# Second attention of a two-layer image transformer: scores and row maxima by halves of 64 rows, with four masked copies of the queries

## The reference

```python
h, s = 8, 16                     # HEADS, HEAD_DIM
q = (x @ Wq.T).reshape(b, t, h, s); k = (x @ Wk.T).reshape(b, t, h, s); v = (x @ Wv.T).reshape(b, t, h, s)
q = _layernorm(q, q_gamma, q_beta)          # over the 16 features of a head
k = _layernorm(k, k_gamma, k_beta)
scores = jnp.einsum('bqhs,bkhs->bhqk', q, k) / jnp.sqrt(s)
scores = jnp.where(cols > rows, -jnp.inf, scores)
attn = jax.nn.softmax(scores, axis=-1)
out = jnp.einsum('bhqk,bkhs->bqhs', attn, v).reshape(b, t, e)
return out @ Wo.T + bo
```

## Time and profile before

| | us |
|---|---|
| median of 3 runs | 2328.66 |
| lowest and highest | 2323.18, 2329.88 |
| profiled execution, its time | 2333.29 |
| its span in the profile | 2331.6 |
| PE busy | 1835.8 |
| DVE busy | 1339.7 |
| ACT busy | 1211.4 |
| POOL busy | 1161.9 |

### The profile page before, as it was taken

One profiled execution on the slowest core, in us unless ns is written; L12 is line 12 of the kernel. 1 busy time (PEld: TensorE's weight loads), 2 busy tenths in 40 slices (PEclk: granted clock), 3 DMA queues, 4 the chain that ended last, 5 costly groups with the idle time before them and its releaser, 6 DMA issues. The chain is left out here.

```text
span 2331.6 us, 48836 instructions
## 1 busy us (share of the span) xinstructions
PE 1835.8 (79%) x12709; PEld 1328.7 (57%) x12710; DVE 1339.7 (57%) x5135; ACT 1211.4 (52%) x2915; POOL 1161.9 (50%) x1035
## 2 busy tenths in 40 slices
PE   5888888872158874998797979797988459998996
PEld 3555555551136552665565656565655359998985
DVE  3788888855541104888777777777776422222222
ACT  2555555530025432876666666666665135555553
POOL 2344444413038872245545454545454448777776
PEclk8999999985569886999999999999999679999998
DMA  9777777610014332011111111111111057776775
GB/s 205 176 191 188 189 189 189 181 29 15 19 45 71 62 46 64 23 40 41 39 34 39 35 38 35 38 35 38 34 34 29 25 118 137 134 136 122 134 134 84
DMA packets 271687, 198.98 MB, mean 85 GB/s; under 512 B 26121, under 2 KB 251947, under 8 KB 271531
## 3 DMA queue, kind: packets, MB, share of 16 engines
q1 hardware_dynamic: 221547, 161.65, 26.8%
q0 software_dynamic: 49984, 35.38, 11.0%
HBM read 144.12 MB, written 52.80 MB: 84 GB/s over the span
## 5 line engine op out<-in xcount | busy, mean ns | idle before, releaser
L2123 POOL DMA_INDIRECT out_dram<-r_yw,r_idx x212 | 328.4, 1549 | 114.9 <-issue 50.4
L2015 POOL DMA_INDIRECT rows_scratch<-routed_row,slot_u x256 | 268.8, 1050 | 124.7 <-issue 72.8
L1691 ACT ACTIVATE a_probsT<-a_p_sc 98x392 f32<-98x392 f32 x384 | 191.9, 500 | 128.0 <-PE a_p_sc L1520 108.0
L2191 ACT ACTIVATE r_hT<-r_p_up,r_b1T 128x256 f32<-128x256 f32 x424 | 190.0, 474 | 115.0 <-PE r_p_up L2165 111.6
L2152 PEld LDWEIGHTS r_p_y<-w_all,r_hT 128*128 128x128 f32 x1696 | 223.3, 192 | 11.1
L2152 PE MATMUL r_p_y<-w_all,r_hT 128*128 x1696 | 224.2, 275 | 0.0
L2165 PE MATMUL r_p_up<-r_xgT,r_w1e 128*128 128x256 f32 x848 | 220.5, 383 | 0.7 <-ACT r_xgT L2196 0.6
L1517 PE MATMUL a_p_sc<-q_head,kT 128*98 128x392 f32 x512 | 218.9, 509 | 0.5 <-ACT q_head L1718 0.5
L407 PE MATMUL p_embed<-pix,w_pix 96*128 96x392 f32 x512 | 211.1, 520 | 4.8 <-ACT pix L533 4.8
L1718 ACT ACTIVATE q_head<-qT,head_of 128x196 f32<-128x196 f32 x512 | 197.1, 467 | 0.0
L650 POOL TENSOR_SCALAR vare<-mv 98x4 f32<-98x4 f32 x64 | 27.9, 436 | 296.9 <-DVE mv L628 215.7
(11 more groups left out here) (361 smaller groups left out, 4535.0 us busy)
## 6 DMA issues: line engine op xcount, KB each, us to landing
img<-in_x_dram SPq DMA_DIRECT2D x192, 196.0 KB, 3.6
img<-in_x_dram SPq DMA_DIRECT2D x192, 189.0 KB, 3.7
r_w1e<-in_L_ffn_W_dram SPq DMA_DIRECT2D x106, 256.0 KB, 3.0
r_xg<-rows_scratch SPq DMA_DIRECT2D x106, 130.0 KB
xn_scratch<-xn SPq DMA_DIRECT2D x32, 196.0 KB
h_scratch<-h SPq DMA_DIRECT2D x32, 196.0 KB
h<-h_scratch SPq DMA_DIRECT2D x32, 196.0 KB
h3b<-h_scratch SPq DMA_DIRECT2D x32, 196.0 KB
```

The source lines that it names most:

```text
L1691: act.activation(probsT[:, r3, m, b * 2 * PAIR:(b + 1) * 2 * PAIR], p_sc[i % 2][:, 0:2 * PAIR], ACT.Exp).then_inc(exped, 1)
L2015: pool.indirect_dma_start(rows_dram, bass.IndirectOffsetOnAxis(ap=slot_u[:, k % 2, c, t:t + 1], axis=0), row[:, k % 2, c, t, :], None).the ...
L2123: pool.indirect_dma_start(acc_dram, bass.IndirectOffsetOnAxis(ap=idx[:, (k - 3) % 4, t:t + 1], axis=0), yw[:, (k - 3) % 4, t, :], None, co ...
L2191: act.activation(hT[:, (k - 1) % 2, f, :], p_up[f][:, 0:G], ACT.Silu, bias=b1T[:, bass.ds(e * FC + f, 1)]).then_inc(act_h, 1)
```

## The change

The queries are written four times instead of once: `q_var[:, slot, v, :]` holds heads v and v+4 and zeros elsewhere, since ACT's activation multiplies and adds by `gains_var`, gains already masked. Partitions 0 to 63 hold heads 0 to 3 and partitions 64 to 127 heads 4 to 7, so that on either half of the partitions variant v has one head alone, and a matmul on 64 rows is exact for it. `q_head`, `k_head_b`, their masks and the bf16 copies are gone; the maxima are computed from the upper halves of the f32 words (`q_high`, `k_high`), read with a step of two.

Banks are handled two at a time: `score_pair(i)` and `max_pair(i)` fill both PSUM banks, one from rows 0 to 63 and one from rows 64 to 127, and wait until both were read. Banks are renumbered: 0 to 3 hold image 0, 4 to 7 the second tiles of both images (for the maxima the first tiles), 8 to 11 image 1. The pairs stand in TensorE's order at (0,1), (2,3), (4,5), (6,7), (8,9), (10,11); bank 6 moves behind the turning of `o_n`, and bank 8 behind the turning of queries and keys and the output projection. An f32 score pair has two matmuls of 392 columns, or four of 196; a maximum pair has four matmuls of 196 columns or eight of 98, and two mask matmuls; auxiliary matmuls are four a pair, 196 columns each. `weigh(0)` waits for 8 exponentials instead of 6.

```diff
-        qT = S("qT", [D, 2, COLS])
+        q_var = S("q_var", [D, 4, LIVE, COLS])
         kT = S("kT", [D, 4, COLS])
-        qT_b = S("qT_b", [D, 2, COLS], BF16)
-        kT_b = S("kT_b", [D, 2, COLS], BF16)
-        q_head = S("q_head", [D, HEADS, COLS])
-        k_head_b = S("k_head_b", [D, 2, HEADS, COLS], BF16)
+        q_high, k_high = q_var[:].bitcast(BF16), kT[:].bitcast(BF16)
...
+                def max_pair(i):
...
+                        done(pe, maxed, 12, u, i)
...
+                    for both in zip(*spans):
+                        for p, (rows, v, q0, k0, size, c) in enumerate(both):
+                            pe.matmul(p_max[p][:, c:c + size], high(q_high, rows, q4, v, (q0, TILE)),
+                                      high(k_high, rows, k4, (k0, size)), start=(c == 0), stop=False,
+                                      skip_group_check=True)
...
+                def score_pair(i):
...
+                        done(pe, exped, 12, u, i)
+                    s4 = (k - 3) % 4
+                    for x in range(2):
+                        for p in range(2):
+                            m, rows, var, _ = places(i + p)
...
+                            elif x == 0:
+                                o = m * PAIR
+                                pe.matmul(p_sc[p][:, 0:2 * PAIR], kT[rows, s4, o:o + TILE],
+                                          q_var[rows, s4, var:var + 2, o:o + PAIR], start=True, stop=False,
+                                          skip_group_check=True)
...
-                banks(4, 7)
+                banks(4, 6)
...
-                banks(7, 9)
+                banks(6, 8)
...
-                banks(9, 10)
+                banks(8, 10)
...
-                split(3, 1, 0, 2)
-                exps(2, 3)
-                split(3, 1, 2, 5)
-                exps(3, 4)
-                split(3, 1, 5, 8)
+                exps(2, 4)
...
+                    for v in range(LIVE):
+                        last = act.activation(q_var[:, (k - 1) % 4, v, :], p_q[0][:, 0:COLS], ACT.Identity,
+                                              bias=gains_var[:, v, 1:2], scale=gains_var[:, v, 0:1])
+                    last.then_inc(qT_ready, 1)
...
-                if on[2]:
-                    masked_keys()
                 maxes(0, 1)
...
+            dve.tensor_tensor(var_of[:], head_of[:, 0:LIVE], head_of[:, LIVE:HEADS], ALU.add).then_inc(wcp, 1)
+            dve.wait_ge(wcp, 2)
+            dve.tensor_tensor(gains_var[:], gains[:, 0:2].unsqueeze(1).to_broadcast([D, LIVE, 2]),
+                              var_of[:].unsqueeze(2).to_broadcast([D, LIVE, 2]), ALU.mult).then_inc(wcp, 1)
```

More of the change, by code:

```diff
@@ L1499, in max_bank @@
-                    last.then_inc(maxmm, 1)
-                def score_bank(i):
+                        done(pe, kT_ready, 1, u)
+                        done(pe, maxed, 12, u - 1)
+                    else:
+                        done(pe, maxed, 12, u, i)
+                    q4, k4 = (k - 2) % 4, (k - 2) % 4
+                    spans = []
+                    for p in range(2):
+                        m, rows, var, _ = places(i + p)
+                        if m is None:
+                            spans.append([(rows, var + j, x * PAIR, x * PAIR, TILE, (2 * x + j) * TILE)
+                                          for x in range(2) for j in range(2)])
+                        else:
+                            spans.append([(rows, var + j, m * PAIR + TILE, m * PAIR, PAIR, j * PAIR)
+                                          for j in range(2)])
@@ L1513, in score_bank @@
[L1513 to L1530, removed]
@@ L1531, in score_bank @@
-                    last.then_inc(scored, 1)
+                        done(pe, exped, 12, u - 1)
+                    else:
+                        done(pe, exped, 12, u, i)
+                    s4 = (k - 3) % 4
+                    for x in range(2):
+                        for p in range(2):
+                            m, rows, var, _ = places(i + p)
+                            if m is None:
+                                o = x * PAIR + TILE
+                                pe.matmul(p_sc[p][:, x * PAIR:(x + 1) * PAIR], kT[rows, s4, o:o + TILE],
+                                          q_var[rows, s4, var:var + 2, o:o + TILE], start=(x == 0), stop=False,
+                                          skip_group_check=True)
[3 more added lines that the diff above has]
+                                          q_var[rows, s4, var:var + 2, o:o + PAIR], start=True, stop=False,
+                                          skip_group_check=True)
@@ new lines, in score_pair @@
+                    for p in range(2):
+                        m, _, _, first = places(i + p)
+                        for par in range(2):
+                            head = aux_l[:, first + par, :]
+                            if m is None:
+                                bank = p_sc[p][:, 0:2 * PAIR].rearrange("p (x h c) -> p x h c", x=2, h=2)
+                                last = pe.matmul(bank[:, :, par, :], head, aux_r[:, r3, :, PAIR:3 * TILE],
+                                                 start=False, stop=True, skip_group_check=True)
+                            else:
+                                last = pe.matmul(p_sc[p][:, par * PAIR:(par + 1) * PAIR], head,
+                                                 aux_r[:, r3, m, 0:PAIR], start=False, stop=True,
+                                                 skip_group_check=True)
+                        last.then_inc(scored, 1)
@@ L1533, in banks @@
                 def banks(lo, hi):
-                    for i in range(lo, hi):
+                    for i in range(lo, hi, 2):
                         if on[3]:
-                            score_bank(i)
+                            score_pair(i)
                         if on[2]:
-                            max_bank(i)
+                            max_pair(i)
                 def qkv_tile(t):
@@ L1707, in tile @@
                              ).then_inc(qkv_act, 1)
[L1709 to L1720, removed]
                 if on[4]:
```

114 lines of the change are left out of this document (41 added, 73 removed).

## The result

The changed kernel takes 2389.4 us (median of 4 runs, 2380.9 to 2392.7), the kernel before, run beside it, 2329.3. The ratio is 1.0265 (95% interval 1.0240 to 1.0289), so it is **slower by 60 us**. I had forecast 2329 and a range up to 2352. The profiled execution has a span of 2379.2 us at a mean clock of 0.886; before it was 2331.6 at 0.904.

The account below looks back on a forecast made before the run. No engine is full; a chain of waits binds, POOL's ring at 27.45 us a unit. Steady units -5.4, jumps +7.5, units behind +5.4, head -3.8, tail -3 sum to +0.7: 2329 us on the median's scale, range 2296 to 2352.

Parts of the forecast that it names:

- The chain at full clock: Second attention, steady unit: the chain of waits between engines sets the time, 27.45 us before and 27.0 after.
- TensorE's ring: Second attention: chain of waits through TensorE and DVE, 25.5 us a unit plus 1.5 from the pairs, 27.0.
- rival A: The forecast itself: the pairs' addition to TensorE's ring takes back what scatters and banks give; 2321 to 2336, chance 0.33.
- B: Faster: DVE's second reduction is absorbed and POOL's 26.0 us ring binds; -33 us, 2296, chance 0.36.
- steady units: Twelve loop units, neither a jump's nor the next one: from 27.45 to 27.0 us each, -5.4 us in all.
- the six units behind the loop's start and its jumps: TensorE waits there for DVE, held 1.82 us in line 1936: 0.9 us lost each, +5.4 in all.
- rival C: Slower clock: if the hole before bank 7's maximum reaches 2.2 us, half the units pay 1.7; +20, 2350, chance 0.19.
- the 4.9 of the sum: TensorE's scores and maxima: the two 64-row halves run side by side and save 4.9 us a unit.
- The jump: Units at the loop's jump back, where POOL is long done, lose the pairs' 1.5 us in full: five, +7.5 us.
- The head: Units ahead of the loop, where TensorE is full and its ring not yet at its length: -3.8 us.
- a change of form: TensorE's switch between half and full rows, 24 a unit: 0.09 us each, 2.2 us a unit; ends 0 and 0.17.
- Rival D: The halves overlap in part (0.33 us a pair, +20, 2349) or not at all (+41, 2370); chance 0.12.

Follow-up runs that it names:

- the kernel with fillers: Changed kernel plus unread TensorE matmuls: six before the turn of the maxima, four before the routed rows, pair (6,7) scores twice; 2339.8 us, ratio 1.0058.
- moving the code: Changed kernel with eight tiny matmuls ahead of TensorE's stage program, nothing added in the loop; 2365.6 us, ratio 1.0159.
- eight copies: Kernel before with eight masked f32 query copies written by ScalarE, no VectorE masks, pairs or 64-row matmuls; 2314.7 us, ratio 0.9942; on the disturbed run 2521.6 us.

## Why the prediction was wrong

*The chain at full clock* was right in kind. TensorE's ring measures 27.12 us (27.0 foretold), the maxima stand 7.8 us behind the queries (7.5), all scatters are at 0.95, the rows no longer wait for rstd, the reduction of bank 0 binds. So rival A's mechanism is what the unit does, and B did not come. That the number fits so well is in part luck: behind bank 0 I had 7.8 - 1.9 = 5.9 us to the next reduction of head variance and there are 5.6, and for what the pairs add I had 1.5 us and there are 1.9 (1.3 up to the turn of the maxima, 0.7 at bank 0, less 0.1). With most of the clock and the second stop out of the way (the kernel with fillers, half clock 48 us, before 61), the loop takes 689.2 us against 694.6 before: steady units -6.8 in all (foretold -5.4), the jumps +6.4 (foretold +7.5), but the six units behind the loop's start and its jumps -5.0, where I had +5.4. I had kept VectorE's 1.82 us in line 1936 there, and they are gone.

*The clock* was the step that failed: the sum has no term for it, and it is worth about 26 us together with what it adds at the jumps. I had given rival C a condition, a single hole that reaches 2.2 us, and found 1.5 in the steady unit. The largest is 1.33, and yet half clock doubled. What the change did was to take work from TensorE (27.12 less its holes is 22.5 us, before 27.45 - 2.16 - 1.17 - 0.35 = 23.8; the 1.3 us are the 4.9 of the sum less 24 changes of 0.15) and to leave six holes, 0.45, 0.97, 0.50, 0.43, 1.33 and 0.98, where there had been three. One stretch at 0.50 after one long hole was too little to read a condition from; C was right in kind and, at 20 us, not far off in size; its condition was wrong.

*The jump* was the second step: +1.5 us each foretold, +4.9 measured. The difference is the second stop and half clock: moving the code brings the jumps to +2.6 each, the fillers to +1.3. The trace of before has no second stop at any jump. I had no bound for "the program's length changes".

*The head* was the third: -3.8 foretold, +11.5 measured. It has two parts. The first two intervals are 5.6 us longer; there TensorE stands 4.10 us, and once more 2.10, ahead of the maxima of a pair, behind reductions that lie among VectorE's root steps, where before the largest hole is 2.53, and half clock rises from 17 to 31 us.

```profile
920.17 0.57 PE L1499 MATMUL a_p_max<-kT,q_var 64*98 64x98 bf16 x8 [4.10 <-DVE a_negmax L1810]
```

The fillers come in only from the fourth interval on, so that the head is as long with them (+11.9) says nothing on the clock in these two; how much of the 5.6 us it is stays open. The other five intervals are 5.9 us longer, all at full clock; with eight copies and no pairs they are longer by 0.2, so this part comes with the pairs on half rows and not with the masked copies. Which of the two, pairs or half rows, isn't shown, and moving bank 1's reduction did not change it. I took TensorE for full in these units, which it is not.

*Mis-sized terms:* a change of form is 0.15 us, not 0.09. Leaving the masks out was worth 36 us, not 17: the twelve steady units give 14.0 us by the traces, but the units behind the loop's start and its jumps give 14.7 more, which I had not counted as going with the masks, and another 11 lie outside the loop. The weighting's 3.97 us should be 3.92, which changes nothing.

*Rival D* fell: records of both halves start 7 ns apart (1354.366 and 1354.373, then 1354.774 and 1354.781), so D's 0.33 us a pair don't come.

The accounts: of the 60 us the second stop is 24 and the clock 26, each to within about 10. The fillers' kernel still has 11 over the kernel before. Its profiled execution is the shortest of its six and only 2.6 us longer than that of before: 12 more in the head, 5 less in the loop, 4 less outside. The other 9 us are in no trace.

## What to carry to other kernels

A change that takes work from TensorE where it is not the bound can lose more clock than the work was worth, as here: look at all its holes in a unit, the small ones too, and price the units at half clock as a term, not as an accident. When a hardware loop's body changes its length, look at the first microseconds behind the jump back, on every engine, before anything else is explained. And when a change brings two things, here masks gone and halves paired, build the one without the other: the first alone made the kernel faster, by 0.6%.

## What the runs showed of the hardware

With matmuls on 64 rows, bank by bank, a unit has a single hole of over 0.3 us on TensorE (0.73, at the turn of the maxima). Half of the 24 intervals in the loop are 31.03 to 31.12 us without any half clock, and yet six take 41.7 to 51.6, of which 24 to 41 us are at 0.50. So a full engine alone doesn't keep the clock. That trace is of the longest of four executions whose times scatter; the shortest, 2537 us, is still above what units of 31.05 us would make (an estimate from the trace: 31.05 in place of the eight long intervals of head and loop and 40 a jump are some 134 us over the kernel before, so about 2460). Why, no other run here shows.

In two of the five batches, those where the kernel before took 2495 us, every unit from the sixth interval on was 6 to 8 us longer in the kernels traced. With eight copies the two conditions differ by 208 us in the profiled executions, 192 of them in the 31 intervals. It is always the same place, here in the kernel with eight copies:

```profile
1603.89 1.04 DVE L1808 TENSOR_REDUCE a_negmax<-a_p_max 98x2 bf16<-98x392 f32 x2 [5.97 <-remote]
1602.44 0.50 ACT L1695 ACTIVATE a_probsT<-a_p_sc 98x392 f32<-98x392 f32 x1 [4.08 <-remote]
1597.58 0.25 PE L1501 MATMUL a_p_max<-mask_qk,ident_b 98*98 98x196 bf16 x1
1605.06 0.41 PE L1668 MATMUL a_p_tr<-ident_b,a_negmax 98*8 98x98 bf16 x3 [7.23 <-DVE a_negmax L1808]
```

VectorE and ScalarE both wait, 5.97 and 4.08 us, for semaphores that TensorE's records of 1596 and 1597 should have raised. The chip was another one the first time, but the second time it was one that had given 2327 us before, so it isn't bound to one chip. What it is stays open.
